# Split float32r products in place of fp32 ones for the first MLP product of three transformer layers

## The reference

```python
y = _ln(x, norm2_g, norm2_b)                     # LayerNorm over the 192 channels
y = gelu(y @ mlp_w1 + mlp_b1) @ mlp_w2 + mlp_b2  # 192 -> 768 -> 192
return x + y
```

## Time and profile before

| | us |
|---|---|
| median of 3 runs | 615.16 (613.29 to 616.64) |
| the profiled execution | 621.33 |
| its span, first to last instruction | 619.5 |
| PE busy in the span | 544.5 |
| mean granted clock, of full speed | 0.932 |

### The profile page before, as it was taken

The page is one execution under the profiler, slowest core; times in us unless marked ns, Lnnn a source line. Parts: engine busy times, 40 slices in busy tenths (PEclk is TensorE's granted clock), DMA queues, the critical chain, the costliest instruction groups (busy, mean ns, idle before and its releaser), DMA issues.

```text
span 619.5 us, 9854 instructions
## 1 busy us (share of the span) xinstructions
PE 544.5 (88%) x3704; PEld 395.4 (64%) x3704; DVE 303.9 (49%) x822; ACT 214.3 (35%) x425; POOL 107.6 (17%) x169
## 2 busy tenths in 40 slices
PE   7987878789989989998979999989877779899997
PEld 6746766666545756656656956747575557565676
DVE  4758686371221723774756431246774962600143
ACT  4314555432343034433434051341343644222110
POOL 5203010130003403314310061110300110300020
PEclk9999879699989999999999999979967796899999
DMA  5981443514213563473473046016515422200001
GB/s 155 222 202 23 104 93 68 157 46 109 55 39 90 133 153 92 114 173 87 108 184 107 1 105 134 0 33 138 108 27 106 91 42 79 64 1 0 1 1 52
DMA packets 22213, 54.13 MB, mean 87 GB/s; under 512 B 5026, under 2 KB 10906, under 8 KB 22070
## 3 DMA queue, kind: packets, MB, share of 16 engines
q1 hardware_dynamic: 21950, 53.40, 36.1%
q10 hardware_dynamic: 216, 0.10, 0.1%
HBM read 10.94 MB, written 0.79 MB: 19 GB/s over the span
## 4 chain that ended last, share of the span: by engine, by line
PE 63%; DVE 16%; DMA 7%; SPq 5%; issue 4%; ACT 2%; POOL 1%; DVEq 0%; ACTq 0%; POOLq 0%
PE PS L1218 61%; DMA QA<-REL 5%; DVE NM L1109 5%; PE PS L1234 2%; DVE HL L1122 1%; DVE OT L1146 1%; DMA PT<-in_qm 1%; DVE OT L1144 1%; DMA QA<-NR 1%; SPq L667 1%; SPq L733 1%; DVE REL L1096 1%; SPq L668 1%; DVE HL L1126 1%; SPq L718 1%
## 5 line engine op out<-in xcount | busy, mean ns | idle before, releaser
L1109 DVE TENSOR_REDUCE NM<-PS 98x2 f32<-98x392 f32 (+2 forms) x192 | 105.3, 569 | 74.2 <-PE PS L1218 72.4
L958 ACT ACTIVATE PT<-PS 98x392 f32<-98x392 f32 (+2 forms) x192 | 94.0, 521 | 98.5 <-PE PS L1218 94.5
L1218 PE MATMUL PS<-KA,QA 126*98 126x196 f32 (+3 forms) x432 | 97.8, 325 | 28.4 <-DVE NM L1109 17.4
L1218 PEld LDWEIGHTS PS<-KA,QA 126*98 126x98 f32 (+3 forms) x432 | 65.5, 194 | 54.2 <-DVE NM L1109 31.1
L1218 PE MATMUL PS<-QA,KA 128*98 128x196 f32 (+2 forms) x480 | 94.5, 312 | 5.0 <-ACT PT L958 3.2
L1218 PEld LDWEIGHTS PS<-QA,KA 128*98 128x98 f32 (+2 forms) x480 | 74.2, 203 | 14.9 <-ACT PT L958 5.6
L1218 PE MATMUL PS<-XT,WQKV 96*96 96x512 f32 x128 | 64.6, 639 | 5.3 <-issue 4.1
L1218 PE MATMUL PS<-XT,W 96*128 96x512 f32 x144 | 65.2, 607 | 3.4 <-issue 3.4
L1218 PE MATMUL PS<-PT,V 128*32 128x196 f32 (+2 forms) x672 | 54.2, 373 | 0.0
L1218 PE MATMUL PS<-W,HT 128*128 128x192 f32 x288 | 48.7, 328 | 4.7 <-ACT HT L984 4.7
L1218 PEld LDWEIGHTS PS<-W,HT 128*128 128x128 f32 x288 | 46.6, 190 | 9.6 <-ACT HT L984 9.6
(11 more groups left out here) (103 smaller groups left out, 657.6 us busy)
## 6 DMA issues: line engine op xcount, KB each, us to landing
QA<-QHL SPq DMA_DIRECT2D x36, 192.0 KB
KA<-KHL SPq DMA_DIRECT2D x24, 228.0 KB
QA<-REL SPq DMA_DIRECT2D x24, 224.0 KB
QA<-QHL SPq DMA_DIRECT2D x12, 384.0 KB
KA<-KHL SPq DMA_DIRECT2D x12, 384.0 KB
KA<-PT SPq DMA_DIRECT2D x12, 380.0 KB
W<-in_w SPq DMA_DIRECT2D x6, 576.0 KB, 5.3
QA<-REL SPq DMA_DIRECT2D x48, 64.0 KB
```

The lines of the kernel that those rows point to most:

```text
L958: nc.scalar.activation(dst, src, ACT.Exp).then_inc(probs_done.sem, 1)
L1109: nc.vector.tensor_reduce(dst, src, AX.X, ALU.max, negate=True).then_inc(max_done.sem, 1)
L1218: return nc.tensor.matmul(dst, lhsT, rhs, start=start, stop=stop, skip_group_check=loose)
```

## The change

What follows holds for all three layers.

- `W1` is loaded as before into a new tile `W1R`, now as 128 rows by 2: channels 0 to 127, and channels 128 to 191 twice. POOL makes of it `W1[:, 0]`, rounded to float32r, and `W1[:, 1]`, the rest, also float32r: a cast and a subtraction of 128 x 1536 elements each, at the step `weights`.
- The turn of the second norm is no transpose but a product with the identity (128 output rows, then 64 rows twice, at partitions 0 and 64), so 12 fp32 products in place of 8 transposes. ACT writes `XR` (float32r) in two instructions, then waits for the split weights, then writes the same values in float32 to `XF` in two more. DVE subtracts and writes the low parts: `XLO` for channels 0 to 127, and for channels 128 to 191 into rows 64 to 127 of `XR[:, 1]`.
- A unit of `up` is five float32r products of 128 rows and 512 columns, in three steps: `up_hi` (high times high, low weights times high tokens), `up_lo` (high weights times `XLO`), and `up` (the channels 128 to 191, high and low tokens in one product, with high and with low weights). The product of low with low of channels 0 to 127 is left out.
- The order of half 0 is new: `up_hi` of four units, `up_lo` of four, `up` of four with their `gelu`, two whole units, and only then half 1's turn, in banks 0 and 1, ahead of `down`.

```diff
-    out += [("up", m, 0, 4 + m) for m in range(2)] + [("turn", 1, 1, 2)]
-    out += [("gelu", m, 0, 4 + m) for m in range(2)]
-    out += [(step, m, 0, (m + 2) % 4) for m in range(2, FM) for step in ("up", "gelu")]
+    banks = (4, 5, 2, 3, 6, 7)
+    out += [(step, m, 0, banks[m]) for step in ("up_hi", "up_lo") for m in range(4)]
+    out += [(step, m, 0, banks[m]) for m in range(4) for step in ("up", "gelu")]
+    out += [(step, m, 0, banks[m]) for m in range(4, FM) for step in ("up_hi", "up_lo", "up", "gelu")]
+    out += [("turn", 1, 1, 0)]
     out += [("down", t, 0, 4 + t % 4) for t in range(4)]
-    out += [(step, m, 1, m % 4) for m in range(FM) for step in ("up", "gelu")]
+    banks = (2, 3, 0, 1, 2, 3)
+    out += [(step, m, 1, banks[m]) for m in range(FM) for step in ("up_hi", "up_lo", "up", "gelu")]
...
+            elif step == "weights":
+                w, full = m["W1"], m["W1R"][:, :, :]
+                pool.wait_ge(*mlp_in.at(n, 1))
+                nc.gpsimd.tensor_copy(w[:, 0, :, :], full).then_inc(w1_hi.sem, 1)
+                pool.wait_ge(*w1_hi.at(n, 0))
+                nc.gpsimd.tensor_tensor(w[:, 1, :, :], full, raw(w[:, 0, :, :]), ALU.subtract)\
+                    .then_inc(w1_lo.sem, 1)
...
+                if s:
+
+                    act.wait_ge(*w1_lo.at(n, 0))
+                    nc.scalar.activation(m["XF"][:, 0, :], PS[:, bank, :], ACT.Identity,
+                                         scale=g[:, 0:1], bias=g[:, 2:3]).then_inc(x_full.sem, 1)
+                    nc.scalar.activation(m["XF"][64:128, 1, :], PS[64:128, bank + 1, :], ACT.Identity,
+                                         scale=g[64:128, 1:2], bias=g[64:128, 3:4]).then_inc(x_full.sem, 1)
...
+            elif step == "turn" and i == 1:
+
+                cols, low = slice(u * 512, (u + 1) * 512), slice(64, 128)
+                parts = [(m["XLO"][:, cols], m["XF"][:, 0, :], XR[:, 0, cols]),
+                         (XR[low, 1, cols], m["XF"][low, 1, :], XR[low, 1, cols])]
+                for k, (lo, full, hi) in enumerate(parts):
+                    dve.wait_ge(*x_full.at(n, 2 * u + k))
+                    nc.vector.tensor_tensor(lo, full, raw(hi), ALU.subtract).then_inc(xlo_done.sem, 1)
...
+                        if s:
+
+                            pe.wait_ge(*xn_done.at(n, TILES + 4 * u + t))
+                            for row, ch in ((0, slice(0, 128)),) if k == 0 else ((0, slice(128, C)), (64, slice(128, C))):
+                                last = mm(PS[row:row + ch.stop - ch.start, bank + k, t * 128:(t + 1) * 128],
+                                          XN[:, 4 * u + t, ch], IDN[:, :], True, True)
+                            continue
...
+            elif step == "up_hi":
...
+                pe.wait_ge(*xt_done.at(n, 4 + 2 * u))
                 claim(bank, gelu_done.at(n, FM * u + i))
...
+                mm(PS[:, bank, :], m["W1"][:, 0, 0, ff], XR[:, 0, cols], True, False)
+                if i == 0 and u == 0:
+                    pe.wait_ge(*w1_lo.at(n, 0))
+                mm(PS[:, bank, :], m["W1"][:, 1, 0, ff], XR[:, 0, cols], False, False)
+            elif step == "up_lo":
+                ff, cols = slice(i * 128, (i + 1) * 128), slice(u * 512, (u + 1) * 512)
+                pe.wait_ge(*xlo_done.at(n, 2 * u))
+                mm(PS[:, bank, :], m["W1"][:, 0, 0, ff], m["XLO"][:, cols], False, False)
+            elif step == "up":
+                ff, cols = slice(i * 128, (i + 1) * 128), slice(u * 512, (u + 1) * 512)
+                pe.wait_ge(*xlo_done.at(n, 2 * u + 1))
+                mm(PS[:, bank, :], m["W1"][:, 0, 1, ff], XR[:, 1, cols], False, False)
+                mm(PS[:, bank, :], m["W1"][:, 1, 1, ff], XR[:, 1, cols], False, True).then_inc(up_psum.sem, 1)
```

More of the change, by code:

```diff
@@ L424, in _build @@
     OS = XNOS[:, 0:NT].rearrange("p (k t) -> p k t", k=2)
-    XT = sb(ctx, "XT", [CK, 2, NT])
+    with ExitStack() as shared:
+        XT = sb(shared, "XT", [CK, 2, NT])
+    XR = sb(ctx, "XR", [128, 2, NT], F32R)
     IDN = sb(ctx, "IDN", [128, 128])
@@ L477, in _build @@
         m["HT"] = sb(frame, f"HT{n}", [128, FM, NT])
-        m["W1"] = sb(frame, f"W1_{n}", [CK, 2, FF])
+        m["W1"] = sb(frame, f"W1_{n}", [128, 2, 2, FF], F32R)
         m["W2"] = sb(frame, f"W2_{n}", [128, FM, C])
+        with ExitStack() as shared:
+            m["W1R"] = sb(shared, f"W1R{n}", [128, 2, FF])
+        m["XLO"] = sb(frame, f"XLO{n}", [128, NT], F32R)
+        m["XF"] = sb(frame, f"XF{n}", [128, 2, 512])
         frame.close()
@@ L745, in _ @@
                     sp.wait_ge(*wait)
-                sp.dma_start(m["W1"][:, :, :], io[f"w1_{n}"]).then_inc(mlp_in.sem, 16)
+                sp.dma_start(m["W1R"][:, :, :], io[f"w1_{n}"]).then_inc(mlp_in.sem, 16)
                 sp.dma_start(m["W2"][:, :, :], io[f"w2_{n}"]).then_inc(mlp_in.sem, 16)
@@ L889, in _ @@
                 s = i
-                g = COL[n][0:CK, 4 * s:4 * s + 4]
+                rows = 128 if s else CK
+                g, x = COL[n][0:rows, 4 * s:4 * s + 4], XR if s else XT
                 if n and s + u == 0:
@@ L894, in _ @@
                     act.wait_ge(*xt_psum.at(n, 4 * s + 2 * u + k))
-                    nc.scalar.activation(XT[:, k, u * 512:(u + 1) * 512], PS[0:CK, bank + k, :], ACT.Identity,
+                    nc.scalar.activation(x[:, k, u * 512:(u + 1) * 512], PS[0:rows, bank + k, :], ACT.Identity,
                                          scale=g[:, k:k + 1], bias=g[:, 2 + k:3 + k]).then_inc(xt_done.sem, 1)
+                if s:
[4 more added lines that the diff above has]
+                                         scale=g[64:128, 1:2], bias=g[64:128, 3:4]).then_inc(x_full.sem, 1)
             elif step in ("q", "k"):
@@ L1418, in _ @@
                     last.then_inc(proj_psum.sem, 1)
-            elif step == "up":
+            elif step == "up_hi":
                 if i == 0 and u == 0:
                     pe.wait_ge(*mlp_in.at(n, 1))
-                pe.wait_ge(*xt_done.at(n, 4 + 2 * u + 1))
+                    pe.wait_ge(*w1_hi.at(n, 0))
+                pe.wait_ge(*xt_done.at(n, 4 + 2 * u))
                 claim(bank, gelu_done.at(n, FM * u + i))
[L1424 to L1427, removed]
+                ff, cols = slice(i * 128, (i + 1) * 128), slice(u * 512, (u + 1) * 512)
[8 more added lines that the diff above has]
+            elif step == "up":
+                ff, cols = slice(i * 128, (i + 1) * 128), slice(u * 512, (u + 1) * 512)
+                pe.wait_ge(*xlo_done.at(n, 2 * u + 1))
+                mm(PS[:, bank, :], m["W1"][:, 0, 1, ff], XR[:, 1, cols], False, False)
+                mm(PS[:, bank, :], m["W1"][:, 1, 1, ff], XR[:, 1, cols], False, True).then_inc(up_psum.sem, 1)
             elif step == "down":
@@ L1507, in _pack @@
         at = 0
-        for v, parts in ((g1, CK), (o1, CK), (g2, CK), (o2, CK), (bqkv[:2 * L.dim], CK), (b1, 128)):
-            c = cols(v, parts)
+        for v, parts in ((g1, CK), (o1, CK), (g2, 128), (o2, 128), (bqkv[:2 * L.dim], CK), (b1, 128)):
+            c = cols(v if len(v) % parts == 0 else twice_last(v), parts)
             col[:parts, at:at + c.shape[1]] = c
@@ L1521, in _pack @@
         arrays |= {f"col{n}": col, f"wqkv{n}": rows(wqkv, CK), f"wp{n}": place.reshape(128, L.groups, C),
-                   f"rb{n}": rb.reshape(CK, 2, L.rel, L.per_chunk), f"w1_{n}": rows(w1, CK),
+                   f"rb{n}": rb.reshape(CK, 2, L.rel, L.per_chunk), f"w1_{n}": rows(twice_last(w1), 128),
                    f"w2_{n}": rows(w2, 128), f"vb{n}": bqkv[2 * L.dim:], f"b2_{n}": b2,
```

9 lines of the change are left out of this document (7 added, 2 removed).

## The result

The changed kernel takes 599.99 us (median of 4 runs, 599.01 to 604.32) against 614.59 of the kernel before (4 runs, 613.29 to 616.64) on the same chip. The recorded ratio is 0.9735, 95% interval 0.9674 to 0.9796; the two medians by themselves divide to 0.976, which lies inside it. Two later comparisons of the same kernel gave 0.9726 (0.9669 to 0.9783) and 0.9702 (0.964 to 0.9764). Medians here are over all runs and ratios over the fast ones, without those that lie over 1.5% above the fastest of the same kernel.

The account below looks back on a forecast made before the run. PE was taken to bound the MLPs. Second halves -11.5 and first halves -7.8 make -19.3 us, the collision +5.0, together -14.3: from a median of 615.16 to 601 us, range 594 to 608.

Parts of the forecast that it names:

- the products: Float32r products of `up`: 0.216 us each, a unit 1.08 instead of 1.72; second halves -11.5 us in three layers.
- the first halves: From an MLP's turn to its first `down`: -2.7 us in layers 0 and 2, -2.4 in layer 1.
- the collision: Layer 1, last head: POOL's weight subtraction holds DVE, PE idles 3.5 us, low clock adds 1.5; together +5.0 us.
- layer 2's clock: Low clock in layer 2's first half: its loss was left in, though the new order might save up to 1.7 us.
- Turns: Second norm's turn: wide products 0.11 us, narrow ones 0.058 by overlapping; 1.8 us a turn against 0.87 before.
- DVE subtracts for `HL`, held by POOL's subtraction: Layer 1's last head: DVE's 0.17 us subtraction at 333.62 waits until POOL's ends at 337.2; PE loses 3.5 us.
- an `HL` of 0.17 in that place: Sign against the forecast: layer 1's last `HL` subtraction keeps 0.17 us, where over 3 us was expected.
- No collision: Rival: in layer 1 `HL` subtraction and POOL's miss each other or the wait is absorbed; 596 us, chance 0.20.
- Dearer turns and handovers: Rival: narrow products in the turns do not overlap, +0.85 us a turn, and `XLO` comes later; about 606, chance 0.14.
- Clock lost in the MLPs: Rival: new PE waits in the MLPs halve the clock, costing 3.4 us in a layer; 608 to 611, chance 0.08.
- No faster: Rival: a 512-column float32r product in `up` takes fp32's 0.43 us, a unit 2.15; 639 us, chance 0.04.
- much faster products: Rival: 512 columns in `up` at 0.131 us, a unit 0.66, gelu pacing second halves; 594 us, chance 0.02.

Follow-up runs that it names:

- the halves: The changed kernel with the second, third and fourth product of each unit issued as two of 256 columns; second half 8.08 us (one run).
- two products fewer: The changed kernel without both products with the low weights of channels 128 to 191 and of XR's first part; 599.61 us, ratio 0.9657 to the kernel before.
- the split on top of the last head: The changed kernel with POOL's weight split waiting for PE's last scores of the maxima; 597.44 us, ratio 0.9654 to the kernel before.

## Why the prediction was right

The time and the main mechanism were right. Four terms were mis-sized: the products (1.8 us too much gain), the first halves (0.7 too much), the collision (2 too much loss on average) and layer 2's clock (1.7 of gain left out). That the median came within 1 us of the forecast is in part luck, since these nearly cancel, and one step, which instruction is held, was wrong. The profile of the change was to be about 607 by the prediction, by adding the 6.2 us that before's lay above its median; it took 599.19.

- **Products.** Mis-sized: 0.2315 us each, not 0.216; the bounds of 0.215 and 0.244 held. (The Trainium skill, TensorE: Matmul & The Clock Gate, Back-to-back issue gap, gives 0.131 for a stream and 0.216 for one alone; the trace agrees with neither for float32r.) A unit is 1.16 in place of 1.08, and a second half gave -3.2, not -3.8: -9.7 us in three layers where the sum had -11.5. I took the lower end because fp32 instructions show no weight loading; the halves show that loading is not what the columns pay. No row spoke for the lower end: in before's trace the 256-column products of the earlier trace rows's shape start a median of 0.120 apart (134 gaps), and twice that is 0.240. The measured price lies a little above the middle of my two bounds.
- **Turns.** The first takes 2.34 us to the first product of `XR` and the second 2.08 with its tail; in a turn that waits for nothing the last instruction starts at 1.80. Both prices hold, 0.111 for a wide one and 0.055 for a narrow one. What the sum left out is the last one's 0.27 and, in the first turns of layers 0 and 2, 0.2 of waits between tiles of `XN`.
- **First half.** -2.47 and -2.2 in layers 0 and 1, predicted -2.7 and -2.4. That ACT ends it is shown by two products fewer, which change nothing. It waits 0.51 there, not 1.2, since PE's stream is slower and uses up what ACT leaves; gelu's start is 0.35 later than I had it (8.75 us behind the turn's start against 8.4). The wait for `XLO` is 0.3, not 0.5 (0.519 between two starts, less 0.232). Dearer products thus cost nothing in this half.
- **Layer 2's clock.** I left its loss in. It is gone: no first half of layer 2 in twelve profiles with float32r products has low clock, both profiles with fp32 products have 3.4 us of it. That gives 1.7 more. Why it falls there and not here was not tested; with the changed order and fp32 products it still fell.
- **The rule of the collision.** The step "DVE subtracts for `HL`, held by POOL's subtraction" failed in the instruction and in the size: it is the cast ahead of it that is held, and in the profiled execution by 1.2 us, not 3.5. By the prediction's own sign ("an `HL` of 0.17 in that place") this step was wrong: the subtraction took 0.17. W2's issue came 1.3 us earlier against the last head's cast than in before's trace (319.33 to 328.74 is 9.4 us, where 325.33 to 333.42 is 8.1), and the split began 5.8 us after the issue of W2, not 6.7. Over eight profiles the term is +3.0, with 1.2 to 4.4, where I had +5.0; the low clock that I added behind the stall came in six, at 0.8 or 1.8 in place of 1.5. I could have read the rule from before's trace, where POOL's instructions hold the same cast in other heads, for 1.10 us at 212.39, 0.38 at 308.89, and here, to 0.03 us behind POOL's end:

```profile
263.80 1.14 DVE L1122 CAST HL<-NM 128x8 fp32r<-128x8 f32 x1
```
```profile
262.54 2.37 POOL L828 TENSOR_TENSOR KHL<-KD,KHL 96x1024 fp32r<-96x1024 f32 x1
```

  The Trainium skill (SBUF — State Buffer, Who interferes with whom) says that the side that starts first keeps the shared ports for its whole instruction, and counts casts among the DVE instructions that can take them; the trace agrees, with DVE's cast ending 0.03 us behind POOL's instruction (330.13 against 330.10). The prediction rested only on its sentence on two inputs.
- **Rivals.** No collision: out, the cast was held in eight of eight. Dearer turns and handovers: of it only the tail and the waits above. Clock lost in the MLPs: out, it was 1.00 in all of them. No faster and much faster products: out.

The terms as measured are -9.7 (second halves), -7.1 and the clock's -1.7 (first halves), +3.0 (collision): -15.5 us, forecast -14.3, the medians of the first comparison say -14.6, and the ratios of three comparisons say -16 to -18 of some 617. If the ratios are right, one to three us are not explained term by term; low clock in layer 2's attention, 41 to 44 us in both profiles with fp32 products and 31 to 41 in those with float32r, is a candidate that was not tested.

## What to carry to other kernels

A stage in which one engine's work shrinks by a third should be read for its next limit in each half by itself: here the same products were worth their full price in one half and nothing in the other, where a statistic queued behind two subtractions held everything. Work given to an idle engine is not free if another engine shares its way to SBUF: look for every short instruction of the other engine in that span, casts too, and put the long one where nothing waits for what it holds. The trace of the kernel before can show which instructions are held: compare each one's longest time with its usual one. And when a term depends on who comes first, give it the mean over arrival times, not the worst row.

## What the runs showed of the hardware that was not expected

- A float32r product of 512 columns starts every 0.2315 us (144 of `XR` and 36 of `XLO`), one of 256 every 0.118: 0.443 ns a column at full clock, 6% above half of what the fp32 instruction takes (0.84).
- fp32 products to output rows 0 to 63 and 64 to 127 start 0.007 us apart when they alternate, and the next two 0.109 later. Eight after eight, the second series still starts while three of the first are to come.
- A DVE cast of 128 x 8 with one SBUF input was held up to 3.17 us by a POOL subtraction. Transposes and reciprocals from SBUF were not: in the kernel with the split on top of the last head they ran at 0.69 and 0.25 us under POOL's 3.49, while the 128 x 512 product of two SBUF operands behind them took 1.56 in place of 0.69.
- ACT's gelu of 128 x 512 takes 0.69 us alone and 0.60 in a run (3.58 for six).
